# Issuing layer 0's expert weights from GpSimd's queue instead of SyncE's, in a two-layer attention and mixture-of-experts kernel

## Chip, cores and metric

The kernel runs on one core of a Trainium2 chip. The metric is device microseconds (us) for one execution, the median of several runs. The kernel before takes 235.27 us (three runs, 234.79 to 235.73).

## What is computed

The input x holds 8 batches of 128 tokens with 128 features; a context holds 8 batches of 128 rows with 96 features. Two layers follow each other, and each adds an attention block and an expert block to x:

```
x = x + cross_attention_0(layernorm(x), ctx)   # 16 heads of 8 features, softmax over 128 context rows
x = x + experts_0(layernorm(x))                # router picks the best 1 of 8 experts per token
x = x + cross_attention_1(layernorm(x), ctx)
x = x + experts_1(layernorm(x))                # gates on the best 2 of 8 experts, all 8 computed
```

In layer 0 an expert is y = square(relu(x fc_e)) proj_e, with fc_e and proj_e of 128 x 512 floats each. That is 256 KB for either matrix and 4 MB for the eight pairs. They lie in HBM and must be in SBUF before the first tile of experts_0 is computed.

## The kernel before

All work is fp32. TensorE (PE) does the products, VectorE (DVE) the maxima and norms, ScalarE (ACT) the exponentials and the copies out of PSUM, GpSimd (POOL) the inverse square roots, some additions and the indirect transfers. SyncE (SP) computes nothing and issues most transfers.

**Attention of layer 0.** It goes batch by batch; a batch is called a row, b = 0 to 7. The steps are counted by n, two for each row. In step n PE forms the scores of row n/2 (L1178), and between these products, in turns, the transposed scores of the row two before it (L1186). DVE takes the row maxima of the scores (L756, tile `mx`). When both steps of row b are done, PE transposes the maxima in step 2b+2 (L1219), ACT copies them to the tile `mT` (L573) and counts the semaphore `m_sb` up. SP, which waits for it (L303), then issues an 8 KB transfer from `mT` into spare partitions of `q4` (L304, `q<-mT`), called the shift row here: with it the transposed scores come out of the product with the maximum already subtracted. PE waits for the landing of the shift row of row b (semaphore `t_row`) ahead of step 2b+4, and with it wait that step's scores, since PE takes its instructions in order. From that step on the row's exponentials (L566) and its products with the values (L1235) follow.

**The weights of layer 0's experts.** In `shift_rows` SP issues them behind the shift rows: behind each of rows 3, 4, 5 and 6 come two experts, which are four transfers of 256 KB (L315 and L316). All 16 count up the one semaphore `s_fc`. ACT waits for the whole count before the first copy of an expert's matrix (L656), well behind the attention. Behind row 7 SP issues the 512 KB of `b2` for layer 1 (L328), then a row of zeros (L331).

**GpSimd's order.** In the same stretch POOL issues four transfers of 64 KB (L415, `q<-work`: queries of rows 4 to 7), clears a tile (L416), adds a bias to x in two halves (`add_bo`, L400), and then waits for DVE's variances to compute the inverse square roots of the second norm (`rsqrt(1, 0)`, L394). DVE needs these to normalise (L730), and PE transposes the result (L1084). Later POOL issues the indirect transfers that sort tokens into expert slots and their results back (L422 and L430).

Of the kernel before, what the change touches and what calls it, by code (L numbers as in the profile page):

```python
# [66 lines left out]
def build(nc, x_in, ctx_in, wa_in, wr_in, fc_in, proj_in, w1_in, w2_in, b2_in, out):  # L67
# [8 lines left out]
    with ctx:  # L76
        def sb(name, shape, dt=fp32):
            return ctx.enter_context(nc.sbuf_tensor(name, shape, dt))

        def sem(name):  # L80
            return ctx.enter_context(nc.semaphore(name))
# [20 lines left out]
        fc = sb("fc", [P, E, F0])  # L102
        proj = sb("proj", [P, E, C0, D])
# [4 lines left out]
        def wcol(layer, name):  # L108
            if layer == 0 and name in A_AT:
                lo, hi = A_AT[name]  # L110
                return wa[:, lo:hi]
            lo, hi = R_AT[name + str(layer) if name in ("wo", "bo") else name]
            return wr[:, lo:hi]
# [68 lines left out]
        s_fc, s_b2, s_zero = sem("s_fc"), sem("s_b2"), sem("s_zero")  # L182
# [17 lines left out]
        s_ps, s_top, top_clip, m_ps, m_sb = (sem(n) for n in ("s_ps", "s_top", "top_clip", "m_ps", "m_sb"))  # L200
# [17 lines left out]
        gathered = [sem(f"gathered{h}") for h in range(2)]  # L218

        CONSTS = 7  # L220
        SB = lambda l, j: 4 * B * l + j + 1
        BB = lambda l, b: l * B + b + 1
        y_bank = lambda layer, half: ((2, 1), (OUT_A_BANK, 7))[layer][half]
# [53 lines left out]
        @block.sync  # L277
        def _(sp):
            sp.dma_start(ctxT[:, 0:512], ctx_in[:, 0:512]).then_inc(s_ctx[0], 16)
            sp.dma_start(wa[:, 0:A_FIRST], wa_in[:, 0:A_FIRST]).then_inc(s_wa, 16)  # L280
            sp.dma_start(xr[:, HB:B, :], x_in.rearrange("(b t) d -> t b d", t=L)[:, HB:B, :]).then_inc(s_x[1], 16)
            sp.dma_start(ctxT[:, 512:1024], ctx_in[:, 512:1024]).then_inc(s_ctx[1], 16)
            sp.dma_start(wr[:], wr_in).then_inc(s_wr, 16)

            def empty_slots(h):
                sp.wait_ge(pool_const, CONSTS)
                sp.wait_ge(tok_base, 1)
                sp.dma_start(slots_x[h].rearrange("(p t) d -> p t d", p=P),
                             xs[:, HT * h:HT * h + HT, :]).then_inc(s_zero, 16)

            def queries_in():
                sp.wait_ge(q_sb, Q_DONE[1])
                for g in range(4):
                    sp.dma_start(q4[32 * g:32 * g + DH, :, 0:512], q_dense[32 * g:32 * g + 32, 0, :]).then_inc(q_in[1], 16)

            def keys_in(part, lo, hi):
                for g in range(4):
                    sp.dma_start(k4[32 * g:32 * g + DH, :, lo:hi],
                                 k_dense[32 * g:32 * g + 32, lo - 256:hi - 256]).then_inc(k_in[part], 16)

            def shift_rows(layer):
                for b in range(B):
                    sp.wait_ge(m_sb, BB(layer, b))  # L303
                    sp.dma_start(q4[DH:P:32, :, L * b:L * b + L], mT[:, b % TRR, :]).then_inc(t_row[b % TRR], 16)  # L304
                    if layer == 0 and b == 0:
                        sp.wait_ge(k_sb, 6)
                        keys_in(1, 512, 1024)
                    if layer == 1 and b == 0:
                        sp.wait_ge(fc_rdy, TILES)
                        sp.wait_ge(yt_ps, TILES)  # L310
                    if layer == 1 and b >= 1:
                        expert_weights(b - 1)
                    if layer == 0 and 3 <= b < 7:
                        for e in (2 * b - 6, 2 * b - 5):
                            sp.dma_start(fc[:, e, :], fc_in[:, e, :]).then_inc(s_fc, 16)  # L315
                            sp.dma_start(proj[:, e], proj_in[:, e]).then_inc(s_fc, 16)  # L316

            def expert_weights(e):
                sp.dma_start(w1[:, e, :], w1_in[:, e, :]).then_inc(s_w12[e], 16)
                sp.dma_start(w2[:, e], w2_in[:, e]).then_inc(s_w12[e], 16)  # L320

            empty_slots(0)
            empty_slots(1)
            sp.wait_ge(k_fill, 1)
            sp.wait_ge(k_sb, 5)
            keys_in(0, 256, 512)
            shift_rows(0)
            sp.dma_start(b2[:], b2_in).then_inc(s_b2, 16)  # L328
            sp.wait_ge(zero_rdy, 1)
            sp.wait_ge(st_ps, 2 * B)  # L330
            sp.dma_start(q4[DH:P:32, :, 0:N // 2], zero_rows[:]).then_inc(q_zeroed, 16)  # L331

            def slots_in(h):
                sp.wait_ge(scattered[h], 16 * HB)
                for i, (lo, hi) in enumerate(XS_PARTS):
                    sp.dma_start(xs[:, HT * h + lo:HT * h + hi, :],
                                 slots_x[h].rearrange("(t p) d -> p t d", p=P)[:, lo:hi, :]).then_inc(xs_in[h][i], 16)

            def outputs_in():
                for i in range(YR):  # L340
                    sp.wait_ge(y_out[0][i], 16 * ((HT + YR - 1 - i) // YR))
                sp.dma_start(yg[:, 0:HB, :],
                             moe_y[0][0:HB * L, :].rearrange("(b p) d -> p b d", p=P)).then_inc(gathered[0], 16)

            slots_in(0)
            slots_in(1)
            outputs_in()
            queries_in()
            shift_rows(1)
            expert_weights(E - 1)  # L350
            for half in range(2):
                sp.wait_ge(x_exp, E * (half + 1))
                sp.wait_ge(b2_added, E * (half + 1))
                sp.dma_start(out.rearrange("(b t) d -> t b d", t=L)[:, 4 * half:4 * half + 4, :],
                             xr[:, 4 * half:4 * half + 4, :]).then_inc(s_out, 16)
            sp.wait_ge(s_out, 32)
# [3 lines left out]
        def _(pool):  # L360
# [30 lines left out]
            def rsqrt(k, half):  # L391
                pool.wait_ge(ln_var, 2 * k + half + 1)
                sl = slice(4 * half, 4 * half + 4) if k else slice(6 * half and 2, 2 + 6 * half)
                nc.gpsimd.tensor_tensor(rstd[:, sl], ve[:, sl], minus_half[:, sl], ALU.pow).then_inc(ln_rstd, 1)  # L394

            def add_bo(layer, half):
                pool.wait_ge(s_wr, 16)
                pool.wait_ge(ln_norm, 4 * layer + half + 1)
                sl = slice(4 * half, 4 * half + 4)
                nc.gpsimd.tensor_tensor(xr[:, sl, :], xr[:, sl, :],  # L400
                                        wcol(layer, "bo").unsqueeze(1).to_broadcast([P, 4, D]),
                                        ALU.add).then_inc(bo_added, 1)
# [13 lines left out]
            nc.gpsimd.memset(zero_rows[:], 0.0).then_inc(zero_rdy, 1)  # L416
            add_bo(0, 0)
            add_bo(0, 1)
            rsqrt(1, 0)

            def scatter(b):
# [49 lines left out]
        def _(act):  # L471
# [89 lines left out]
            def attention(layer):  # L561
                def exp(j):
                    act.wait_ge(st_ps, SB(layer, j))
                    if SB(layer, j) > PTR:
                        act.wait_ge(o_ps, SB(layer, j) - PTR)
                    nc.scalar.activation(PT[:, j % PTR, :], ps[:, ST_BANK(layer, j), :], ACT.Exp,  # L566
                                         scale=SCALE).then_inc(b_done, 1)
# [7 lines left out]
                def o_evac(b):  # L575
                    act.wait_ge(o_ps, SB(layer, 4 * b + 3))
                    if layer * B + b >= 2:
                        act.wait_ge(t_ps, layer * B + b - 1)
                    nc.scalar.activation(osb[:, b % 2, :], ps[:, 6, 0:256], ACT.Copy).then_inc(o_sb, 1)
# [123 lines left out]
        def _(dve):  # L703
# [48 lines left out]
            def attention(layer):  # L752
                def tops(j):
                    dve.wait_ge(s_ps, SB(layer, j))
                    b, g = divmod(j, 4)
                    nc.vector.tensor_reduce(mx[:, b, 4 * g:4 * g + 4], ps[:, S_BANK(layer, j), :].rearrange("p (k m) -> p k m", m=M),  # L756
                                            axis=AX, op=ALU.max).then_inc(s_top, 1)

                def clip_tops(b):
                    dve.wait_ge(s_top, SB(layer, 4 * b + 3))  # L760
                    nc.vector.tensor_scalar(mx[:, b, :], mx[:, b, :], CLAMP, FLOOR_SHIFT, ALU.min, ALU.max).then_inc(top_clip, 1)
# [826 lines left out]
```

## Time and profile before

| | |
|---|---|
| median of three runs | 235.27 us |
| lowest, highest | 234.79, 235.73 us |
| the profiled execution's own time | 235.83 us |
| its span, from first to last instruction | 234.1 us |
| PE busy | 218.1 us, 93% |
| DVE, ACT, POOL busy | 163.2, 123.9, 78.4 us |
| granted TensorE clock | 1.00 over the whole span |

The span leaves 1.73 us of the profiled execution's time outside. That execution lies 0.56 us above the median. A row of a timeline gives the start, the duration, the engine, the line, the operation, and what is written and read; several like instructions in a row are merged, with their count behind x, and a bracket gives the idle time before them and what ended it. "SPq" marks instructions of SP that issue a transfer. "DMA to landing" is the time from the start of an issue to the last count of its semaphore.

### The profile page before, as it was taken

To read this page: it belongs to the slowest core of one execution; us is meant where nothing else is said; L and a number is where in the kernel's file an instruction comes from. 1 tells how busy PE (TensorE), PEld (TensorE's weight loads), DVE (VectorE), ACT (ScalarE), POOL (GpSimd) and SP (SyncE) were. 2 spreads that over 40 slices of the span, in tenths; PEclk is the share of its full clock that TensorE was granted. 3 is DMA by queue.
4 is the path that set the end of the run, shared out by engine and by line. 5 is a ranking of instruction groups with operands and counts; after the bars stand their busy time and mean duration, and the time that the engine had idled before them with its cause. 6 is when DMAs were issued, how large, how long until landed. Compare 5 with 4: busy or idle time off the path is not lost.

```text
span 234.1 us, 6754 instructions
## 1 busy us (share of the span) xinstructions
PE 218.1 (93%) x2534; PEld 171.2 (73%) x2534; DVE 163.2 (70%) x513; ACT 123.9 (53%) x236; POOL 78.4 (33%) x104
## 2 busy tenths in 40 slices
PE   8899987999998999999978789999699999999993
PEld 8766866777566999998875566877568686776772
DVE  1676766864754875559438875898758965799994
ACT  6665554655584565565620467666563276244240
POOL 8810810001251277746351794756600100000000
PEclk9999999999999999999999999999999999999999
DMA  6932118671014016120122110222300000001001
GB/s 217 349 142 54 49 46 278 226 246 41 0 46 126 0 61 171 56 83 22 48 69 60 46 51 4 74 70 54 91 1 3 0 0 0 3 1 46 3 0 45
DMA packets 13780, 16.85 MB, mean 72 GB/s; under 512 B 1604, under 2 KB 9924, under 8 KB 13748
## 3 DMA queue, kind: packets, MB, share of 16 engines
q1 hardware_dynamic: 11396, 13.26, 18.5%
q0 software_dynamic: 1152, 2.24, 3.1%
q10 hardware_dynamic: 1200, 0.92, 1.2%
q8 instruction: 21, 0.34, 0.6%
q14 instruction: 11, 0.09, 0.1%
HBM read 11.38 MB, written 3.95 MB: 65 GB/s over the span
## 4 chain that ended last, share of the span: by engine, by line
PE 71%; DVE 14%; DMA 5%; ACT 3%; issue 3%; POOL 2%; DVEq 0%; ACTq 0%; POOLq 0%; SPq 0%
PE ps L1397 12%; PE ps L1385 12%; PE ps L1178 10%; PE ps L1468 5%; PE ps L1478 5%; PE ps L1235 5%; DVE mx L756 4%; PE ps L1186 4%; PE ps L1070 3%; PE ps L1425 2%; PE ps L1249 2%; DVE xn L730 2%; PE ps L1139 2%; DMA q<-work 2%; PE ps L1273 2%
## 5 line engine op out<-in xcount | busy, mean ns | idle before, releaser
L756 DVE TENSOR_REDUCE mx<-ps 128x4 f32<-128x512 f32 x64 | 41.0, 685 | 18.0 <-PE ps L1178 17.7
L566 ACT ACTIVATE PT<-ps 128x512 f32<-128x512 f32 x64 | 35.6, 590 | 25.5 <-PE ps L1186 25.5
L1178 PE MATMUL ps<-k,q 32*128 32x128 f32 x512 | 35.9, 282 | 4.2 <-DMA q<-mT 1.3
L1178 PEld LDWEIGHTS ps<-k,q 32*128 32x128 f32 x512 | 30.6, 186 | 12.6 <-DVE mx L756 8.9
L1186 PE MATMUL ps<-q,k 32*128 32x128 f32 x512 | 34.9, 283 | 0.3 <-DVE mx L756 0.3
L1397 PEld LDWEIGHTS ps<-proj,work 128*128 128x128 f32 x256 | 30.7, 192 | 5.7 <-issue 5.7
L694 ACT ACTIVATE work<-ps,fc 128x512 f32<-128x512 f32 x32 | 21.3, 687 | 24.1 <-PE ps L1385 22.7
L1397 PE MATMUL ps<-proj,work 128*128 128x128 f32 x256 | 31.1, 275 | 0.0
L1186 PEld LDWEIGHTS ps<-q,k 32*128 32x128 f32 x512 | 29.2, 186 | 1.8 <-issue 1.6
L430 POOL DMA_INDIRECT moe_y<-ys,tok_i x22 | 22.2, 1009 | 24.0 <-DVE ys L986 12.0
L1385 PE MATMUL ps<-xT,fc 128*128 128x512 f32 x64 | 30.1, 593 | 0.0
L1478 PE MATMUL ps<-proj,work 128*128 x176 | 24.4, 282 | 0.8 <-DVE ys L986 0.8
L995 DVE TENSOR_TENSOR work<-work 128x512 f32<-128x512 f32 x22 | 15.2, 691 | 14.2 <-ACT work L672 14.2
L1468 PE MATMUL ps<-xsT,work 128*128 128x128 f32 x176 | 23.4, 276 | 0.0
L1478 PEld LDWEIGHTS ps<-proj,work 128*128 128x128 f32 x176 | 21.3, 191 | 1.9 <-issue 1.1
L1031 DVE SCALAR_TENSOR_TENSOR xr<-ps,gates,xr 128x128 f32<-128x128 f32 x64 | 18.1, 343 | 6.4 <-PE ps L1397 5.0
L466 POOL TENSOR_SCALAR PT<-PT 128x512 f32<-128x512 f32 x32 | 19.2, 620 | 9.9 <-ACT PT L566 9.7
L672 ACT ACTIVATE work<-ps 128x512 f32<-128x512 f32 x22 | 13.1, 597 | 17.0 <-PE ps L1468 17.0
L394 POOL TENSOR_TENSOR rstd<-ve,minus_half 128x4 f32<-128x4 f32 (+2 forms) x8 | 8.3, 1032 | 40.2 <-DVE ve L721 40.2
L1468 PEld LDWEIGHTS ps<-xsT,work 128*128 128x128 f32 x176 | 21.4, 192 | 0.3 <-issue 0.3
L1235 PE MATMUL ps<-PT,vaug 128*32 128x128 f32 x512 | 19.4, 278 | 0.0
L1049 DVE SCALAR_TENSOR_TENSOR xr<-b,gates,xr 128x128 f32<-128x128 f32 x64 | 18.1, 347 | 1.1
(168 smaller groups left out, 310.9 us busy)
## 6 DMA issues: line engine op xcount, KB each, us to landing
fc<-in_fc SPq DMA_DIRECT2D x8, 256.0 KB, 3.4
proj<-in_proj SPq DMA_DIRECT2D x8, 256.0 KB, 4.0
slots_x<-xs SPq DMA_DIRECT2D x2, 709.5 KB, 7.7
fc<-in_w SPq DMA_DIRECT2D x8, 129.0 KB, 2.3
proj<-in_w SPq DMA_DIRECT2D x8, 128.0 KB, 3.5
wr<-in_wr SPq DMA_DIRECT2D x1, 913.0 KB, 8.1
xs<-slots_x SPq DMA_DIRECT2D x2, 322.5 KB, 3.6
xs<-slots_x SPq DMA_DIRECT2D x2, 258.0 KB, 3.0
```

Of the source, the lines that this page charges most:

```text
L430: pool.indirect_dma_start(moe_y[h], bass.IndirectOffsetOnAxis(tok_i[:, t:t + 1], 0), ys[:, t % YR, :], None).then_inc(y_out[h][t % HT % YR ...
L466: nc.gpsimd.tensor_scalar(PT[:, j % PTR, :], PT[:, j % PTR, :], 1.0, FLOOR, ALU.min, ALU.max).then_inc(p_clamp, 1)
L566: nc.scalar.activation(PT[:, j % PTR, :], ps[:, ST_BANK(layer, j), :], ACT.Exp, scale=SCALE).then_inc(b_done, 1)
L694: nc.scalar.activation(hT[:, idx % 2, c, :], ps[:, UP_BANK[idx % 2][c], :], ACT.Gelu, bias=w1[:, e, F1 + c:F1 + c + 1]).then_inc(hT_rdy, 1)
L756: nc.vector.tensor_reduce(mx[:, b, 4 * g:4 * g + 4], ps[:, S_BANK(layer, j), :].rearrange("p (k m) -> p k m", m=M), axis=AX, op=ALU.max).t ...
L1178: ins = mm(ps[:, S_BANK(layer, 2 * n + i), P * k:P * k + P], q4[r:r + 32, k, L * b:L * b + L], k4[r:r + 32, k, M * b:M * b + M], start=Tru ...
L1186: ins = mm(ps[:, ST_BANK(layer, 2 * m + i), P * k:P * k + P], k4[r:r + 32, k, M * b:M * b + M], q4[r:r + 32, k, L * b:L * b + L], start=Tr ...
L1235: ins = mm(ps[32 * k:32 * k + 32, 6, 128 * c:128 * c + 128], vaug[:, b, 4 * g + k, :], PT[:, j % PTR, 128 * k:128 * k + 128], start=first, ...
L1385: mm(ps[:, UP_BANK[idx % 2][c], :], w1[:, e, P * c:P * c + P], xT[:, 512 * half:512 * half + 512], start=True, stop=True).then_inc(up_ps, 1)
L1397: ins = mm(ps[:, DN_BANK[idx % 2], P * i:P * i + P], hT[:, idx % 2, c, P * i:P * i + P], w2[:, e, c, :], start=(c == 0), stop=(c == C1 - 1))
L1468: ins = mm(ps[:, H_BANK[t % 2], P * c:P * c + P], fcb[:, t % 2, P * c:P * c + P], xsT[:, t % 2, :], start=True, stop=True)
L1478: ins = mm(ps[:, Y_BANK, 0:D], h2[:, t % 2, P * c:P * c + P], proj[:, bass.ds(expert, 1), c, :].rearrange("p a d -> p (a d)"), start=(c == ...
```

## The change

The loop over L313 to L316 goes out of SP's program. A loop over the eight experts comes into GpSimd's, between `add_bo(0, 1)` and `rsqrt(1, 0)`. Before each expert GpSimd waits for the maxima of a row: row 1 for expert 0, row 2 for experts 1 and 2, row 3 for expert 3, row 4 for experts 4 and 5, row 5 for expert 6, row 6 for expert 7. What is transferred, into which tiles and on which semaphore, stays the same.

```diff
+        FC_ROW = (1, 2, 2, 3, 4, 4, 5, 6)
...
                     if layer == 1 and b >= 1:
                         expert_weights(b - 1)
-                    if layer == 0 and 3 <= b < 7:
-                        for e in (2 * b - 6, 2 * b - 5):
-                            sp.dma_start(fc[:, e, :], fc_in[:, e, :]).then_inc(s_fc, 16)
-                            sp.dma_start(proj[:, e], proj_in[:, e]).then_inc(s_fc, 16)
...
             add_bo(0, 0)
             add_bo(0, 1)
+            for e, b in enumerate(FC_ROW):
+                pool.wait_ge(m_sb, BB(0, b))
+                pool.dma_start(fc[:, e, :], fc_in[:, e, :]).then_inc(s_fc, 16)
+                pool.dma_start(proj[:, e], proj_in[:, e]).then_inc(s_fc, 16)
             rsqrt(1, 0)
```

## Rows read from the trace of the kernel before

**Rows 1.** The page: busy time of PE, and the chain's shares by engine.

```profile
PE 218.1 (93%) x2534; PEld 171.2 (73%) x2534; DVE 163.2 (70%) x513; ACT 123.9 (53%) x236; POOL 78.4 (33%) x104
...
PE 71%; DVE 14%; DMA 5%; ACT 3%; issue 3%; POOL 2%; DVEq 0%; ACTq 0%; POOLq 0%; SPq 0%
```

**Rows 2.** The chain that ended last, 36 to 40 us: start, us, what.

```profile
35.98 0.28 ACT mT L573
...
36.27 3.14 DMA q<-mT
39.41 0.09 issue
```

**Rows 3.** Waits, 31 to 53 us: us in total, times, longest.

```profile
PE ps L1178 <- DMA q<-mT: 1.3, 1, 1.3
```

**Rows 4.** Timeline of SP's queue, 27 to 51 us.

```profile
27.25 5.49 SPq L304 DMA_DIRECT2D q<-mT  x2
32.78 0.45 SPq L315 DMA_DIRECT2D fc<-in_fc  x1
33.28 1.66 SPq L316 DMA_DIRECT2D proj<-in_proj  x1
34.99 0.43 SPq L315 DMA_DIRECT2D fc<-in_fc  x1
35.46 0.43 SPq L316 DMA_DIRECT2D proj<-in_proj  x1
...
41.59 0.53 SPq L304 DMA_DIRECT2D q<-mT  x1
...
45.65 0.53 SPq L304 DMA_DIRECT2D q<-mT  x1
...
49.83 0.53 SPq L304 DMA_DIRECT2D q<-mT  x1
```

**Rows 5.** Timeline of PE, the products at which a row's transposed scores begin.

```profile
34.18 0.38 PE L1178 MATMUL ps<-k,q 32*128 32x128 f32 x2
...
39.50 0.38 PE L1178 MATMUL ps<-k,q 32*128 32x128 f32 x2 [1.30 <-DMA q<-mT]
...
43.56 0.38 PE L1178 MATMUL ps<-k,q 32*128 32x128 f32 x2
...
47.86 1.16 PE L1186 MATMUL ps<-q,k 32*128 32x128 f32 x16
...
52.39 1.16 PE L1186 MATMUL ps<-q,k 32*128 32x128 f32 x16
```

**Rows 6.** Windows: stretch, us, busy of each engine, PE clock, DMA share, GB/s.

```profile
37.00:40.00 3.00, 1.70 (x56) 1.34 (x52) 1.63 (x4) 1.36 (x3) 0.00 (x0) 1.00 0.91 312
```

**Rows 7.** POOL: line L415's summary (ns min/median/max), then its timeline.

```profile
L415 POOL DMA_DIRECT2D q<-work x4: 547/554/845, 24.6 to 26.5; - x4
...
27.52 2.49 POOL L400 TENSOR_TENSOR xr<-xr,wr 128x512 f32<-128x512 f32 x2
52.73 1.04 POOL L394 TENSOR_TENSOR rstd<-ve,minus_half 128x4 f32<-128x4 f32 x1 [22.72 <-DVE ve L721]
...
66.85 0.96 POOL L422 DMA_INDIRECT slots_x<-xn,slot_i  x1 [0.30 <-issue]
```

**Rows 8.** POOL's transfers at L430, 87.5 to 94 us and then 114 to 123 us.

```profile
DMA to landing us min/median/max: 2.2/2.7/3.7
...
DMA to landing us min/median/max: 2.2/2.2/2.2
```

**Rows 9.** SP's three loads at L336, 69 to 71 us and then 88 to 91 us.

```profile
DMA to landing us min/median/max: 2.3/3.0/3.5
...
DMA to landing us min/median/max: 2.3/3.1/3.7
```

**Rows 10.** Timeline of all engines, 55 us; then line L656's summary.

```profile
55.27 0.54 PEld L1084 LDWEIGHTS ps<-ident,xn 128*128 128x128 f32 x4 [0.49 <-DVE xn L730]
...
L656 ACT ACTIVATE work<-fc x22: 616/632/636, 67.7 to 115.8; 128x512 f32 x22
```

## Prediction

> **What bounds the kernel now.** I began with the page. PE is busy 93% of the span and holds 71% of the chain that ended last [rows 1], so time can be won here only where PE stands still, or where something late moves PE's work. Then I followed the chain through layer 0's attention, where the change acts. One transfer stands in it: the shift row of row 4, issued at 36.27 us as soon as ACT had written the maxima, landed at 39.41 us, which is 3.14 us later [rows 2]. The waits confirm it: over 31 to 53 us PE waits once for a shift row, for 1.30 us [rows 3, 5]. The timeline of SP's queue says why that one: before it four weight transfers of 256 KB were issued from 32.78 us on, the last two only 1.3 and 0.8 us ahead of it [rows 4]; the DMA engines were 91% busy, at 312 GB/s, from 37 to 40 us [rows 6].
>
> How much time does a shift row have? From its issue to the product that needs it: row 3 is the second issue in its merged row, which ends at 27.25 + 5.49 = 32.74 us and takes 0.53, so it starts at 32.21, and PE's product starts at 34.18: 1.97 us. Row 4: PE was ready at 39.50 - 1.30 = 38.20: 1.93 us. Row 5: 43.56 - 41.59 = 1.97. Row 6: 47.86 - 45.65 = 2.21. Row 7: 52.39 - 49.83 = 2.56 [rows 4, 5]. All but row 4 kept within it, row 3 with no weights ahead of it. How early they landed is not shown; I take 0.2 us of spare time for rows 3 to 5 (so some 1.75 us unhindered) and, by their larger budgets, 0.45 for row 6 and 0.8 for row 7.
>
> **Removed.** SP loses 16 issues; SP was on no chain and the shift rows were issued on time, so the issue time itself is worth nothing. What counts is that a shift row no longer stands behind weights in SP's own queue. That is worth at most the 1.30 us of row 4, the only idle time there is. After it PE works nearly without a gap, and the rest of the kernel hangs on PE, DVE and POOL, so whatever is won moves to the end in full.
>
> **Added on POOL.** 16 issues and 8 waits. The waits for rows 1 and 2 are over when POOL is free, at 27.52 + 2.49 = 30.01 us [rows 7]. The price of one issue isn't in the trace: a transfer of 64 KB at L415 takes 0.55 us, an indirect one over 128 partitions 0.96, or 1.26 with the gap before it [rows 7]. I take 0.96, since the weights fill 128 partitions too, and keep 0.55 and 1.26 as ends. Experts 0 to 2 then go out from 30.0 to 35.8 us, expert 3 to 37.7, experts 4 and 5 to 41.5, expert 6 to 43.4, and expert 7 behind the maxima of row 6, at about 45 (the time of SP's issue less what was won) to 47. At 1.26 the last would end at 30.01 + 16 x 1.26 = 50.2. Behind them on POOL waits the inverse square root, which starts at 52.73 now [rows 7], or 51.4 with 1.3 us won. So it is covered by 4 us, at the worse price by 1.2. If that cover were gone, the loss would be full, since PE already waits 0.49 us for the normalised rows there [rows 10]. ACT needs the weights at 67.7 us [rows 10]; they land some 20 us earlier.
>
> **Moved: the weights' traffic.** This is the term that decides. Before, weights start behind row 3; now they start at 30 us, so rows 3, 4 and 5 are each issued while another queue's weights are moving. 256 KB at 312 GB/s take 0.84 us and the issues come every 0.96, so there is traffic nearly all the time, but little backlog. The price x of a small SP transfer beside POOL's traffic is bounded so: SP's loads at L336, beside POOL's transfers, took 2.3/3.1/3.7 us against 2.3/3.0/3.5 in the first half, so 0 to 0.2 more [rows 9]. The other way round, POOL's 64 KB transfers beside those SP loads took 2.7 in the median and 3.7 at most, against 2.2 without: 0.5 to 1.5 more [rows 8]. I take 0.5: the weights are a denser stream than POOL's transfers of rows 9, and the shift row is a thinner one than those of rows 8. Ends: 0 and 1.5. Each of rows 3 to 5 then stalls PE for 0.5 - 0.2 = 0.3 us, together 0.9; row 6 (0.45 spare) and row 7 not at all.
>
> **The sum.** -1.30 + 0.9 = -0.4 us. On the profiled execution 235.83 - 0.4 = 235.4; that execution is 0.56 above the median, and on the median it makes 235.27 - 0.4 = 234.9 us.
>
> Row 4's landing of 3.14 us behind weights in its own queue [rows 2] is where a rule of the Trainium skill has a word. DMA: Bandwidth & Descriptors, section on issuing engines, says that transfers issued from scalar, sync or gpsimd end up on the same 16 DMA engines and interleave, and that spreading issues saves the sequencer's time alone; by that nothing is won on row 4, and earlier traffic costs on row 3. The same page of the Trainium skill, section on queues and rings, says that each DMA engine takes turns between the queues it has work for, packet by packet; by that row 4 passes the backlog and nearly all of the 1.3 us comes back. The trace has cases near both (rows 8 and 9), and no shift row beside weights from another queue.
>
> **Rivals.**
> (a) *Full gain.* The shift row takes its turn at once, x stays under 0.2 us, no row stalls: 235.27 - 1.30 = 234.0 us. For it: rows 9. Against: rows 8.
> (b) *Slower: the weights of the other queue hold up every shift row.* The mechanism is row 4's wait, now on rows 3, 4, 5 and 6 instead of one. With x = 1.4: 3 x 1.2 + (1.4 - 0.45) + (1.4 - 0.8 = 0.6 on row 7, if expert 7 is still moving, which I halve) = 4.9; less 1.3 it is +3.6, or 238.8 us. It decides from x = 0.9 on, where 3 x 0.7 + 0.45 - 1.3 = +1.25. For it: the 1.5 of rows 8, and 3.14 against 1.75 in rows 2. The Trainium skill, in the page named above, says in the section on completion order that the count which ends a transfer lands only behind all earlier writes of that DMA engine, of whatever queue; that would be a way to it.
> (c) *POOL late.* If one issue costs over (51.4 - 30.0)/16 = 1.34 us, the inverse square roots start late and PE waits; at 1.5 us it is +2.6 - 1.3, or 236.6. It lies outside the prices of rows 7, so it gets little.
> (d) *Nothing moves.* Row 4 lands as late as now, because expert 3's and 4's weights meet it from the other queue, and the other rows keep their budget: 235.3.
>
> **How the numbers follow.** My forecast gets 0.33, (a) 0.33, (b) 0.21, (c) 0.06, (d) 0.07. About 0.5%, or 1.2 us, is what can be told from no change. (a) lies just beyond it: faster 0.33. The forecast and (d) lie within: 0.40. (b) and (c) give slower 0.27. The likeliest single number is the forecast's, 234.9. Low end: (a) less a scatter of 0.3 us, 233.7. High end: x = 1.1, where 3 x 0.9 + 0.65 + 0.3 - 1.3 = +2.35, so 237.6; the upper part of (b) stays out, as 1 to 2 in 10. The forecast's own range is 234.1 to 235.9.
>
> **What would show it.** Right, if the wait of 1.3 us at PE's L1178 for `q<-mT` falls to 0.2 to 0.4 us and like waits appear on two other rows; if POOL's issues at the new lines take about 1 us each; if the inverse square root still waits for DVE and not for POOL's queue; if the DMA share from 31 to 34 us rises and that from 43 to 52 falls. (a) is seen by no wait for `q<-mT` at all, (b) by three or four of about 1 us, (c) by the root beginning right behind the last weight issue. Wrong altogether, if a time moves behind 70 us, where nothing of the change reaches.

## The result, and the profile after

The kernel after takes 241.66 us in the median of 4 runs (240.54 to 243.12), against 235.44 for the kernel before beside it: a ratio of 1.027, 95% interval 1.022 to 1.031. It is slower by 6 us, where 0.4 us less was forecast. The pair was run again later, with 239.98 against 235.62 us (1.016, 1.008 to 1.023). Both times lie above the high end of the forecast, 237.6 us.

The profiled execution took 243.12 us. Its page begins so:

```profile
span 241.2 us, 6754 instructions
...
PE 222.1 (92%) x2534; PEld 174.2 (72%) x2534; DVE 161.6 (67%) x513; ACT 124.0 (51%) x236; POOL 87.5 (36%) x120
...
PEclk9999996899999999999999999999979999999999
...
PE 70%; DVE 11%; DMA 9%; ACT 3%; issue 3%; POOL 2%; DVEq 0%; ACTq 0%; POOLq 0%; SPq 0%
```

Against [rows 1], transfers hold 9% of the chain instead of 5%, and TensorE's granted clock, 1.00 before throughout, falls in the seventh and eighth of the 40 slices (6.03 us each) and once more in the 30th. The waits from 30 to 56 us name the cause of the first part:

```profile
POOL fc L418 <- ACT mT L574: 13.7, 3, 7.7
...
PE ps L1179 <- DMA q<-mT: 4.2, 1, 4.2
```

As in [rows 3] there is one wait for a shift row, but it is 4.2 us long instead of 1.3. The chain says that it is another row, row 3, whose maxima ACT wrote at 32.03 us (before, row 4's stood there, [rows 2]):

```profile
32.03 0.26 ACT mT L574
...
32.30 6.00 DMA q<-mT
38.31 0.09 issue
```

Row 3's shift row was in time before. Now it takes 6.00 us. POOL's timeline shows what went ahead of it:

```profile
30.04 0.61 POOL L418 DMA_DIRECT2D fc<-in_fc  x1
30.64 0.56 POOL L419 DMA_DIRECT2D proj<-in_proj  x1
31.19 0.55 POOL L418 DMA_DIRECT2D fc<-in_fc  x1
31.73 0.55 POOL L419 DMA_DIRECT2D proj<-in_proj  x1
32.26 0.55 POOL L418 DMA_DIRECT2D fc<-in_fc  x1
...
33.88 0.55 POOL L419 DMA_DIRECT2D proj<-in_proj  x1
42.13 0.55 POOL L418 DMA_DIRECT2D fc<-in_fc  x1 [7.70 <-ACT mT L574]
...
58.22 1.04 POOL L391 TENSOR_TENSOR rstd<-ve,minus_half 128x4 f32<-128x4 f32 x1 [5.73 <-DVE ve L722]
...
68.38 1.08 POOL L423 DMA_INDIRECT slots_x<-xn,slot_i  x1 [9.12 <-DVE slot_i L948]
```

An issue costs 0.55 us. The waits for rows 1, 2 and 3 hold nothing back, so eight transfers, 2 MB, leave POOL from 30.04 to 34.43 us. Five of them had been started when SP issued the shift row at 32.30 us, the fifth only 0.04 us ahead of it. Asked one by one, the eight took 3.1, 3.1, 3.8, 4.0, 4.5, 4.8, 4.9 and 5.8 us from issue to landing. So the fifth landed at 36.8 us, the sixth at 37.6 and the seventh at 38.2, and the shift row behind them at 38.30, although the last two of these were issued after it. The windows show the rest (columns: us, busy of each engine with its count, PE clock, DMA share, GB/s):

```profile
34.00:36.00 2.00, 0.24 (x12) 0.00 (x0) 0.72 (x2) 0.89 (x3) 0.43 (x1) 1.00 1.03 308
36.00:38.00 2.00, 0.00 (x0) 0.00 (x0) 0.00 (x0) 0.00 (x0) 0.00 (x0) 0.87 0.91 347
38.00:40.00 2.00, 1.60 (x28) 1.64 (x32) 0.00 (x0) 0.00 (x0) 0.00 (x0) 0.50 0.10 39
...
42.00:44.00 2.00, 2.00 (x36) 1.80 (x32) 0.75 (x3) 0.32 (x1) 1.87 (x4) 0.50 0.33 82
```

The DMA engines move 308 and 347 GB/s, about the 312 of [rows 6] or more. PE has stood since 34.2 us and from 36 us on every compute engine stands. The clock goes from 2.4 to 1.2 GHz (0.50) at 37.5 us, inside the standstill, which ends at 38.40 us. It is back at 44.3 us. The price of that is read from the times at which ACT writes the maxima of rows 3 to 7:

```profile
41.57 0.27 ACT L574 ACTIVATE mT<-ps 16x128 f32<-16x128 f32 x1 [0.41 <-PE ps L1220]
46.78 0.27 ACT L574 ACTIVATE mT<-ps 16x128 f32<-16x128 f32 x1
50.85 0.27 ACT L574 ACTIVATE mT<-ps 16x128 f32<-16x128 f32 x1
```

From row 5 to row 6 it takes 4.07 us, undisturbed. From row 3 to row 4 it takes 41.57 - 32.03 = 9.54: less 4.07, less the wait of 4.16 us, 1.3 are left; from row 4 to row 5 it takes 5.21, so 1.1 more. Together the half clock cost 2.4 us. The balance at the first scatter is then +4.2 (row 3's wait) + 2.4 (clock) - 1.3 (row 4's old wait, which is gone) = +5.3; POOL issues it at 68.38 us against 62.89 before, 5.5 later. The remaining 1.6 us of the span's 7.1 come later. The clock falls again there, and 3.4 us at half of it are of about that size, an estimate and not a measurement:

```profile
174.00:178.00 4.00, 3.83 (x43) 3.03 (x43) 1.05 (x5) 0.95 (x2) 0.04 (x1) 0.57 0.00 0
```

Only one execution was profiled. By the mean clock, two of the four had such a second fall (0.979, 242.4 and 243.1 us) and two had not (0.984 and 0.986, 241.0 and 240.5 us).

### The profile page after: what moved, and what is told of

It reads as the page before. It is cut to its first block, busy times and chain, and to the rows that moved or that the text cites. A ratio compares the mean times of both kernels' runs of the same rounds, so it can differ in the third digit from the quotient of the medians.

```text
span 241.2 us, 6754 instructions
## 1 busy us (share of the span) xinstructions
PE 222.1 (92%) x2534; PEld 174.2 (72%) x2534; DVE 161.6 (67%) x513; ACT 124.0 (51%) x236; POOL 87.5 (36%) x120
## 4 chain that ended last, share of the span: by engine, by line
PE 70%; DVE 11%; DMA 9%; ACT 3%; issue 3%; POOL 2%; DVEq 0%; ACTq 0%; POOLq 0%; SPq 0%
PE ps L1398 12%; PE ps L1386 11%; PE ps L1179 10%; PE ps L1469 5%; PE ps L1236 5%; PE ps L1479 5%; PE ps L1187 3%; PE ps L1071 3%; DMA moe_y<-ys,tok_i 3%; DMA q<-mT 2%; PE ps L1426 2%; DMA work<-moe_y 2%; DVE mx L757 2%; PE ps L1250 2%; DVE xn L731 2%
## 5 line engine op out<-in xcount | busy, mean ns | idle before, releaser
L1179 PE MATMUL ps<-k,q 32*128 32x128 f32 x512 | 37.8, 292 | 8.2 <-DMA q<-mT 4.2
L1179 PEld LDWEIGHTS ps<-k,q 32*128 32x128 f32 x512 | 32.2, 194 | 16.8 <-DVE mx L757 8.6
L1187 PE MATMUL ps<-q,k 32*128 32x128 f32 x512 | 36.7, 292 | 0.3 <-DVE mx L757 0.3
L1187 PEld LDWEIGHTS ps<-q,k 32*128 32x128 f32 x512 | 30.9, 194 | 1.8 <-issue 1.6
L431 POOL DMA_INDIRECT moe_y<-ys,tok_i x22 | 22.7, 1030 | 23.3 <-DVE ys L987 11.4
L1236 PE MATMUL ps<-PT,vaug 128*32 128x128 f32 x512 | 20.5, 290 | 0.0
```

The lines of the kernel that those rows point to most:

```text
L431: pool.indirect_dma_start(moe_y[h], bass.IndirectOffsetOnAxis(tok_i[:, t:t + 1], 0), ys[:, t % YR, :], None).then_inc(y_out[h][t % HT % YR ...
L1179: ins = mm(ps[:, S_BANK(layer, 2 * n + i), P * k:P * k + P], q4[r:r + 32, k, L * b:L * b + L], k4[r:r + 32, k, M * b:M * b + M], start=Tru ...
L1187: ins = mm(ps[:, ST_BANK(layer, 2 * m + i), P * k:P * k + P], k4[r:r + 32, k, M * b:M * b + M], q4[r:r + 32, k, L * b:L * b + L], start=Tr ...
L1236: ins = mm(ps[32 * k:32 * k + 32, 6, 128 * c:128 * c + 128], vaug[:, b, 4 * g + k, :], PT[:, j % PTR, 128 * k:128 * k + 128], start=first, ...
```

## The experiments

**A: the four corners of queue and order.** Is it GpSimd's queue, or the order in which the weights now come? First GpSimd's queue with the rows of before:

```diff
-        FC_ROW = (1, 2, 2, 3, 4, 4, 5, 6)
+        FC_ROW = (3, 3, 4, 4, 5, 5, 6, 6)
```

> The weights go out from GpSimd's queue, as after, but behind the same rows as before: experts 0 and 1 behind row 3, 2 and 3 behind row 4, and so on. Theory A (a shift row gets no turn while GpSimd's queue holds a backlog of weights, so what counts is the backlog when it is issued): row 3 lands in time, as nothing is ahead of it; row 4, issued 4 us behind a burst of 1 MB, meets its last part and PE waits 1 to 2.5 us for it; the time is 235 to 237.5 us, far from the 241.7 us of after. Rival theory B (GpSimd's queue is bad in itself, for whatever hangs on it): still 239 us or more. Rival theory C (the queues take turns and only the start at 30 us hurt): row 4 is in time, 234.0 us.

Then SP's queue with the order and start of after (an edit of the kernel before):

```diff
-                    if layer == 0 and 3 <= b < 7:
-                        for e in (2 * b - 6, 2 * b - 5):
+                    if layer == 0 and b == 2:
+                        sp.wait_ge(bo_added, 2)
+                    for e in {2: (0, 1, 2), 3: (3,), 4: (4, 5), 5: (6,), 6: (7,)}.get(b, ()) if layer == 0 else ():
```

> The weights stay in SP's queue, but with the order and the start of after: SP waits until 30.0 us (both bias additions done) and issues experts 0 to 2 ahead of row 3's shift row, expert 3 behind it, 4 and 5 behind row 4, 6 behind row 5, 7 behind row 6. Theory A: in one queue the shift row stands behind 6 transfers but ahead of expert 3's, so it lands at about 36 us instead of 38.3; PE waits some 2 us for it and the clock does not fall, so 236 to 238 us, better than after although everything is in one queue. Theory D (the queue makes no difference, only the bytes that are in flight near the shift row do): PE waits over 4 us as after, 241 us.

These two, and the first runs of C and of D, were made on a chip on which before takes 243.25 us. With GpSimd's queue and the old rows the ratio is 1.006 (1.002 to 1.010); the chain has row 4's shift row at 2.89 us and, not foreseen, row 6's at 3.82. The waits:

```profile
PEld ps L1187 <- DMA q<-mT: 1.8, 1, 1.8
PE ps L1187 <- DMA q<-mT: 1.6, 1, 1.6
PE ps L1179 <- DMA q<-mT: 1.1, 1, 1.1
```

(The first two lines are row 6's: one wait of PE's two parts. The last is row 4's.) This profile is of the longest of the ten executions, 248.39 us against a median of 245.26, so row 6's wait can't be taken for the kernel's usual one. By the ratio, the new queue with the old rows is near before, not near after. With SP's queue and the new order the ratio is 1.023 (1.018 to 1.029), near after. My number for it (a wait of 2 us, no fall of the clock) missed: PE waited 4.0 us and the clock fell. It is what theory D forecast. Since the slower chip left its doubts, it was run again on one where before takes 235.87 us:

> sp_new_rows again, for a chip on which before takes 235 to 236 us: the order and start of after, in SP's queue. On the slower chip its row 3 took 5.34 us against 5.30 for the same order in GpSimd's queue. If the queue makes no difference, row 3 takes 5 to 6 us, PE waits 3 to 4.2 us, and the ratio is 1.015 to 1.027, the one of after.

Measured: ratio 1.022 (1.017 to 1.029), with this chain and this wait:

```profile
33.00 5.13 DMA q<-mT
...
PE ps L1179 <- DMA q<-mT: 3.8, 1, 3.8
```

It is the loss of after, to within the intervals, with no weight transfer on GpSimd's queue; the clock fell too, and was at half until 44.6 us. The order isn't quite that of after: six transfers went ahead of the shift row, not five. The sixth landed at 37.6 us and the shift row at 38.13. The order, in which weights now go out just ahead of row 3, is the cause of the loss, and the queue isn't.

The kernel before has the same pattern on row 4. Its last weight transfer ahead of the shift row was issued at 35.46 us and landed 3.7 us later, at 39.2; the shift row landed at 39.41 [rows 2].

**B: before and after again.** Is the odd second half of the slower chip the chip's?

> The kernel before, unchanged, profiled beside the runs below. The four runs so far came from a chip on which before takes 243.25 us against 235.4; their profiles show a fall of the granted clock at 90 to 100 us and GpSimd's transfers at L423 taking 3.5 to 4.7 us instead of 2.3. If both belong to the chip (theory K), they stand in the profile of before on such a chip too, and only the stretch up to 60 us is to be compared. If they come from the edits, before shows neither.

> The kernel after, unchanged, beside before on the same chip. If the wait behind row 3's shift row is all there is to it, the profile shows one wait of 4 us for q<-mT at L1179, a fall of the clock right behind it, and the time is 5 to 7 us over before on the same chip.

On this chip before has the clock at 1.00 in all its span of 233.3 us and GpSimd's scatters at 2.3 us to landing, as in the first profile. The kernels of A and C that were run on other chips show no fall at 90 to 100 us either. So the edits are not what brings it. Before was not profiled on the slower chip; its mean clock there, 0.986 in the median of 19 executions (0.999 and 1.00 on the two other chips), fits theory K. Those runs are read by their first 60 us and their ratios alone. Row 4's shift row, 3.14 us in [rows 2], took 2.47 here, with a wait of 0.8 us: the old loss itself varies. The kernel after waited less than the first time, behind the same order, and lost 4.4 us where 5 to 7 were expected:

```profile
32.36 5.06 DMA q<-mT
...
PE ps L1179 <- DMA q<-mT: 3.2, 1, 3.2
```

The clock was at half for 3.4 us (from 37.6 us on) instead of 6.8, and there was no second fall. The fifth weight transfer landed at 37.3 us and the shift row right behind it, at 37.42; the sixth came after it, at 37.9. That is the difference of the two profiles: the first time the shift row came in behind the sixth and the seventh as well.

**C: is the clock's share real?** The kernel after with products that fill PE's standstill; they write into a PSUM bank that the next scores overwrite, and change no result.

```diff
+                    if layer == 0 and n == 10:
+                        for _ in range(8):
+                            mm(ps[:, S_BANK(0, 2 * n), :], ident[:], wcol(0, "wq"), start=True, stop=True)
                     if 0 <= m < 2 * B:
                         scores_t(m)
```

> The kernel after, with 8 products of 512 columns (into a PSUM bank that the next scores overwrite) ahead of the wait for row 3's shift row, so that PE computes during most of the 4.2 us. They only add work. Theory E (the 4.2 us in which PE stood still made the granted clock fall to half until 44.3 us, which cost another 2.6 us, and a second fall at 174 us 1.7 us in half of the executions): the clock is 1.00 throughout and the time falls by 2.5 to 4 us from 241.7, to 238 to 239 us. Rival theory F (the clock fell for another reason, or its fall cost nothing): 241 us or more, since the products can't shorten anything.

The time did not fall: 1.031 (1.025 to 1.037), more than any other. The clock stayed at 1.00 there, but my size was wrong: a product of 512 columns takes 0.89 us, eight took 7.1 us, and PE was at them until 40.84 us, while the DMA engines had been all but still since 39 us. With four:

> As after_pe_filled, with 4 products instead of 8. The 8 took 7.1 us (0.89 each), longer than the wait they were to fill, and so cost 3 us themselves; 4 take 3.6 us, inside the 4.2 us. Theory E (the standstill made the clock fall, and that fall cost some 2.5 us): no fall between 30 and 50 us, and the first scatter at L423 is issued 2 to 3 us earlier than in after_again, counted from the issue of row 0's shift row. Theory F (the fall costs nothing or has another cause): the same time as after_again or later.

```profile
34.51 3.70 PE L1287 MATMUL ps<-wa,ident 128*128 128x512 f32 x8
38.14 0.38 PE L1179 MATMUL ps<-k,q 32*128 32x128 f32 x2
```

(The four products are eight records.) The windows beside it have the clock at 1.00 from 32 to 46 us:

```profile
36.00:38.00 2.00, 2.00 (x6) 0.66 (x4) 0.00 (x0) 0.00 (x0) 0.00 (x0) 1.00 0.89 336
38.00:40.00 2.00, 2.00 (x45) 1.51 (x44) 0.67 (x2) 0.58 (x2) 0.00 (x0) 1.00 0.20 80
```

From row 3's maxima to row 5's it takes 44.00 - 32.35 = 11.65 us, against 44.92 - 32.09 = 12.83 in after_again: 1.2 us won by work that does nothing, although the scores of this step began 0.4 us later (5.79 us behind row 3's maxima, against 5.42). Then row 5's shift row, 0.2 us closer behind the second burst, is late by 0.8 us, so that at row 6's maxima 0.4 us are left. From row 0's shift row to the first scatter it takes 48.94 us against 49.23, 0.3 less where 2 to 3 were expected, and the ratio, 1.013 (1.005 to 1.021) against 1.016, can't tell the two apart. Theory E's mechanism is shown up to row 5, in one profile of either kernel: PE's standstill brings the fall, and the fall costs time. That the whole kernel gains by the filling is not shown. The 2 to 3 us that I expected were too much for a run whose fall lasted 3.4 us.

**D: weights where they hurt no shift row.** If the backlog is the price, spreading must cure it. A first try used the quiet time behind row 1:

```diff
+                    for e in {1: (0, 1), 3: (2,), 4: (3,), 5: (4,), 6: (5,), 7: (6, 7)}.get(b, ()) if layer == 0 else ():
```

> SP's queue, spread: experts 0 and 1 behind row 1 (from 21.5 us, when little moves), one expert each behind rows 3, 4, 5 and 6, and the last two behind row 7. No shift row then has more than 0.5 MB ahead of it, issued some 3.5 us earlier. If the backlog at the time of issue is the whole price (theory A), no shift row is late, PE's wait of 1.30 us for row 4 goes and nothing takes its place: 234.0 to 234.3 us, ratio 0.995. If something else made row 4 late (theory G), the wait stays and the time is 235.4 us.

On the slower chip it gave 1.002 (0.998 to 1.006), with no wait for row 4's shift row but a new one of 2.3 us for row 2's. The 1 MB behind row 1 met the queries that POOL moves at 24 us, and these, on another queue than the weights, took 5.0 us to landing instead of 3.6:

```profile
DMA to landing us min/median/max: 4.9/5.0/5.2
```

The time isn't as quiet as it looked: the weights must keep clear of these queries too. The second try leaves them until row 3 and puts half of them behind row 7:

```diff
+                    for e in {3: (0,), 4: (1,), 5: (2,), 6: (3,), 7: (4, 5, 6, 7)}.get(b, ()) if layer == 0 else ():
```

> SP's queue; one expert (0.5 MB) behind each of rows 3 to 6, and the last four behind row 7, where no shift row follows. sp_spread was faulty at another place: the weights behind row 1 held up the queries that GpSimd moves (5.1 us instead of 3.7 to landing) and row 2's shift row (4.4 us), and PE waited 2.3 us. Theory A (backlog at the time of issue is the whole price, in whatever queue): here no shift row has over 0.5 MB ahead of it, all land within 1.7 us, no wait for q<-mT is left, and the time is 1.3 us under before. Theory G (something else made row 4 late): its wait stays, no change. The weights land by about 58 to 60 us and are needed at 67.7.

It takes 234.34 us against 235.62, a ratio of 0.993 (0.990 to 0.996): faster than both. Among the waits from 30 to 56 us there is none for `q<-mT`. The queue's timeline has the shift rows 4.06 to 4.18 us apart, which is the undisturbed step:

```profile
36.34 0.53 SPq L304 DMA_DIRECT2D q<-mT  x1
36.92 0.45 SPq L314 DMA_DIRECT2D fc<-in_fc  x1
40.41 0.53 SPq L304 DMA_DIRECT2D q<-mT  x1
...
44.47 0.53 SPq L304 DMA_DIRECT2D q<-mT  x1
...
48.65 0.53 SPq L304 DMA_DIRECT2D q<-mT  x1
```

The same spread from GpSimd's queue, with the inverse square roots ahead of the last four experts:

```diff
-        FC_ROW = (1, 2, 2, 3, 4, 4, 5, 6)
+        FC_ROW = (3, 4, 5, 6, 7, 7, 7, 7)
...
             for e, b in enumerate(FC_ROW):
+                if e == 4:
+                    rsqrt(1, 0)
```

> GpSimd's queue with the spread of sp_late: one expert behind each of rows 3 to 6, then the inverse square roots, then the last four experts (8 issues of 0.55 us, from about 52.8 us to 57.2). Theory A (the backlog at the time of a shift row's issue is the whole price, in whatever queue): all shift rows land within 1.7 us, no wait for q<-mT, and the time is that of sp_late, 0.99 to 0.995 of before. Theory B (GpSimd's queue holds up SP's transfers in itself): waits of 0.5 us and more behind rows 3 to 6, and a time at or above before.

234.44 us against 235.87, 0.994 (0.991 to 0.997), and again no wait for a shift row. GpSimd's queue is as good as SP's, and no better.

**E: the dose.** Only expert 0 ahead of row 3:

```diff
-        FC_ROW = (1, 2, 2, 3, 4, 4, 5, 6)
+        FC_ROW = (1, 4, 4, 5, 5, 6, 6, 7)
```

> As after, with rows (1, 4, 4, 5, 5, 6, 6, 7): only expert 0, two transfers, is issued at 30 us, ahead of row 3's shift row, instead of five transfers. Dose: with five ahead the shift row took 5.1 to 6.0 us. If it waits for the bytes ahead (theory A), two transfers, which land at about 33.9 us, leave it at 1.7 to 2.1 us, and PE waits at most 0.2 us there. If any traffic of the other queue costs the whole wait, it takes over 3 us. Behind row 4 come 1 MB, so row 5's or row 6's shift row may be late by 0 to 1.5 us, as row 4's is in before; the time is 234.5 to 237 us.

The time is that of before, 1.000 (0.996 to 1.003). Row 3 is in time behind two transfers; the only wait is a short one further on:

```profile
PE ps L1179 <- DMA q<-mT: 0.2, 1, 0.2
```

The two were issued at 29.51 and 30.11 us and landed at 32.6 and 33.2. The shift row was issued at 31.96, and PE's product that needs it started at 33.92 without a wait. So 0.5 MB, issued 2.4 and 1.9 us ahead, cost row 3 nothing, and 1.25 MB, issued in the 2.3 us ahead, cost it 3 to 4 us.

**F: the shift rows on a queue of their own.** ACT issues layer 0's shift rows, and SP's weights stay as before. The profile counts SP's transfers and ACT's as two queues, both "hardware_dynamic".

```diff
                     nc.scalar.activation(mT[:, b % TRR, :], ps[0:H, 7, 384:512], ACT.Copy).then_inc(m_sb, 1)
+                    if layer == 0:
+                        act.wait_ge(m_sb, BB(0, b))
+                        act.dma_start(q4[DH:P:32, :, L * b:L * b + L], mT[:, b % TRR, :]).then_inc(t_row[b % TRR], 16)
```

> The weights in SP's queue as before, but the shift rows of layer 0 are issued by ACT, which writes mT and has a hardware queue of its own. If two hardware queues take turns, row 4's shift row takes 1.7 to 2.1 us instead of 2.5 to 3.1 behind the same four weight transfers, and its wait is gone. If nothing but the bytes in flight counts (theory A in its strict form), it still takes 2.5 to 3.1 us. ACT pays about 0.5 us of issue for each row, beside its exponentials; the time is 235 to 237 us.

The ratio is 1.011 (1.004 to 1.017), worse than before. Row 4's shift row took 2.76 us, and rows 3, 5 and 6, which were in time in SP's queue, became late as well (in order, rows 3 to 6):

```profile
32.48 3.28 DMA q<-mT
37.94 2.76 DMA q<-mT
42.89 2.60 DMA q<-mT
47.67 2.85 DMA q<-mT
```

Row 3 is the telling one. No weights were ahead of it; SP's first weight issues came at 32.54 and 32.92 us, 0.06 and 0.44 us behind it, since SP no longer issues the shift row first. In before, where SP issued row 3's shift row itself and its first weights 0.57 us later, it was in time. Here it landed at 35.76 us, right behind the first weight transfer (35.5). A queue of its own gave the small transfer no precedence over a large one that started at the same moment. Whether the other queue or the 0.5 us of head start makes that difference was not separated. ACT's own issues, 0.55 us each, are in the time of this run too.

## Why the prediction was wrong

**Where it looked was right.** Row 4's wait of 1.30 us is gone: the waits of after name one shift row, and it is row 3's. POOL's waits for rows 1 and 2 were over, as said. Rival (c) did not happen: the inverse square roots waited 5.73 us for DVE, not for POOL's queue. Row 7 and the weights' own deadline were no matter.

**The step that failed first is POOL's price.** Of the ends 0.55 and 1.26 us I took 0.96, by the 128 partitions; an issue costs 0.55 to 0.61 us, the lower end. At 0.96 the issues would have come more slowly than the data move (0.84 us each); at 0.55 they come faster, so a backlog grows, which the prediction had ruled out ("little backlog"). Experts 0 to 3 were out by 34.4 us instead of 37.7. No run spaced the issues by 0.96 us, so what the lower price alone costs is not measured; E shows that two transfers ahead cost nothing.

**The term that was mis-sized is x.** I bounded it at 0 to 1.5 us by rows where one transfer met another, and took 0.5. The 0.3 us of stall on each of three rows (x less 0.2 us spare) was a stall of 4.16 us on row 3 alone, and of 3.21 in the second profile. Against the assumed 1.75 us unhindered, x was 4.25 and 3.3 us (6.00 and 5.06 less 1.75). Row 4's old wait was the nearer model, and its lesson was not "SP's own queue is in the way" but "the bytes around it are": then five transfers ahead instead of four, packed into 2.3 us and with more close behind, would have been read as worse than row 4. The rows were no three either: with the first burst gone, rows 4 to 7 were in time, so the loss stood on one row.

**Left out: the clock.** Of the time lost up to the first scatter 2.4 us are products at 1.2 GHz behind PE's standstill. No rival had it. In [rows 5] PE had stood 1.30 us without a fall.

**The rivals.** The sign is (b)'s, and so is its way: weights of the other queue hold up a shift row. Its size, 238.8 us, was too small, and it had four small waits where there was one large one. (a) was wrong, and A shows why: its premise was that the shift row takes its turn at once. (d) was wrong too, since row 4 came in time and row 3 did not. Of the two rules of the Trainium skill that I set against each other, the runs side with the one of DMA: Bandwidth & Descriptors, section on issuing engines: pool_late and sp_late tie, and sp_new_rows2 loses what after loses. Both tie and loss are to within the intervals, on different chips in the first case. The turns between queues, which the section on queues and rings describes, may be taken, but a shift row of 8 KB got nothing from them that can be seen: 6.00 and 5.06 us beside GpSimd's queue, 5.13 in the one queue.

**What stays open.** Why the same order costs 4.2 us once and 3.2 us once: the landings say that two more transfers came in ahead of the shift row the first time, but not why; and why the clock falls a second time at 174 us in some executions of after. Nothing was tried on either. The views show when the shift row's last count lands, not on which of the 16 DMA engines it stood, nor whether its bytes or only that count came late.

## What to carry to other kernels

In this kernel a small transfer that an engine waits for was held up by the large ones issued shortly ahead of it or together with it, on whatever queue. Moving the large ones to another queue won nothing, and moving them in time did. One queue at least keeps the order: a small transfer issued first in it was in time (row 3 in before), and on separate queues it was not (F). Count the bytes that are issued shortly before each small transfer: here 0.5 MB behind each one cost nothing, 1 MB behind each cost 0.8 to 1.3 us on one row of before, and 1.25 MB right ahead cost 3 to 4 us. A wait that is met long ago is no brake: a loop whose gates are already open issues everything in one burst.

## What the runs showed of the hardware

- GpSimd issues a plain transfer over 128 partitions of 2 KB in 0.55 us, while 256 KB take about 0.84 us to move at 312 GB/s; so GpSimd alone can fill the DMA engines (share 0.91 to 1.03 in the windows above).
- TensorE's clock fell to half in a standstill of 4.2 us and 0.1 us behind one of 3.2 us, and stayed there for 6.8 and 3.4 us, for 2.4 and 1.5 us of lost time (the second by the same working: 40.66 - 32.09 - 4.07 - 3.2 = 1.3, and 0.2 on the next row). With PE kept busy over the same stretch it did not fall.
- A late shift row of 8 KB landed within 0.5 us of the last 256 KB transfer issued ahead of it, in one queue (before, before_again, sp_new_rows2) as beside GpSimd's (after_again, pool_one_ahead). In pool_old_rows it was 0.8 us behind it, and in the first profile of after 1.5 us.
- Two queues, ACT's with an 8 KB transfer and SP's with 256 KB ones behind each other, started within 0.06 us of each other: the small one took 3.28 us.
- One chip of those used was 3% slower for the unchanged kernel (243.25 us against 235.4 to 235.9).
